# The copy of the input into the accumulator of the first expert layer, in one piece and in two halves

## The reference, cut to what matters

```
x = x + 0.5 * ffn(layernorm(x))
x = x + attention(layernorm(x))
x = x + 0.5 * ffn(layernorm(x))

ffn:  xn = x * rsqrt(mean(x*x) + eps) * norm_weight
      probs = softmax(xn @ router_w.T + router_b)
      gates, idx = top_k(probs.T, 2048)          # each of 8 experts takes its best 2048 rows
      ye = gelu(xn[idx] @ fc1.T + b1) @ fc2.T + b2
      out = scatter_add(ye * gates, idx) / sum of a row's gates
```

## Time and profile before

| what | value |
|---|---|
| median of 3 runs | 2059.93 us (2059.39 to 2060.3) |
| profiled execution | 2061.12 us |
| its span, first to last instruction | 2059.3 us |
| mean granted clock of TensorE in the span | 0.979 of 2.4 GHz |
| busy share: PE, DVE, ACT, POOL | 95%, 70%, 68%, 61% |

### The profile page before, as it was taken

One profiled execution on the slowest core, in us unless ns is written; L12 is line 12 of the kernel. 1 busy time (PEld: TensorE's weight loads), 2 busy tenths in 40 slices (PEclk: granted clock), 3 DMA queues, 4 the chain that ended last, 5 costly groups with the idle time before them and its releaser, 6 DMA issues.

```text
span 2059.3 us, 42658 instructions
## 1 busy us (share of the span) xinstructions
PE 1955.1 (95%) x15442; PEld 1358.3 (66%) x15442; DVE 1448.4 (70%) x4307; ACT 1399.0 (68%) x2680; POOL 1264.6 (61%) x1428
## 2 busy tenths in 40 slices
PE   8868999999999998799999999869999999999997
PEld 6635666666666665577777777536666666666665
DVE  7788877677777763489989998778655656556542
ACT  8645676666766764578888787556667666666663
POOL 8232788888888784544444443024887777766755
PEclk9979999999999999899999999989999999999999
DMA  9943555555657453556555554224565555655433
GB/s 288 336 143 100 101 101 98 119 98 106 107 94 129 73 81 62 103 121 162 160 159 145 155 149 113 96 72 116 101 121 101 101 102 95 130 93 100 74 60 42
DMA packets 361746, 242.34 MB, mean 118 GB/s; under 512 B 228929, under 2 KB 348993, under 8 KB 361281
## 3 DMA queue, kind: packets, MB, share of 16 engines
q1 hardware_dynamic: 304192, 172.34, 32.7%
q0 software_dynamic: 57344, 67.29, 21.6%
HBM read 121.03 MB, written 84.93 MB: 100 GB/s over the span
## 4 chain that ended last, share of the span: by engine, by line
PE 81%; DVE 5%; issue 5%; ACT 4%; POOL 2%; DMA 2%; SPq 1%; DVEq 0%; POOLq 0%; ACTq 0%
PE ps L1513 25%; PE ps L1514 25%; PE ps L1515 25%; ACT zt_l L734 2%; PE ps L1739 2%; ACT zt_h L734 1%; PE ps L1613 1%; PE ps L1686 1%; DVE bst L1015 1%; POOL xe L596 1%; PE ps L1768 1%; DMA xa<-x_d 0%; POOL out L618 0%; PE ps L1694 0%; PE ps L1731 0%
## 5 line engine op out<-in xcount | busy, mean ns | idle before, releaser
L1289 DVE SCALAR_TENSOR_TENSOR hid_l<-hf,hid_h 128x512 f16<-128x512 f32 x512 | 348.6, 691 | 310.2 <-ACT hid_h L734 308.9
L1513 PE MATMUL ps<-w_h,hid_h 128*128 128x256 f16 x2048 | 558.8, 273 | 3.9 <-DVE hid_l L1289 3.9
L1514 PE MATMUL ps<-w_l,hid_h 128*128 128x256 f16 x2048 | 558.8, 273 | 0.0
L1515 PE MATMUL ps<-w_h,hid_l 128*128 128x256 f16 x2048 | 558.8, 273 | 0.0
L834 ACT ACTIVATE hf<-ps,b 128x512 f32<-128x512 f32 x512 | 346.4, 677 | 137.8 <-PE ps L1515 105.8
L1513 PE MATMUL ps<-xt,w_h 128*128 128x512 f16 x1024 | 388.6, 380 | 13.5 <-ACT hf L834 9.1
L1515 PE MATMUL ps<-xt,w_l 128*128 128x512 f16 x1024 | 388.6, 379 | 0.0
L1514 PE MATMUL ps<-xt,w_h 128*128 128x512 f16 x1024 | 388.6, 379 | 0.0
L734 ACT ACTIVATE hid_h<-hf 128x512 f16<-128x512 f32 x512 | 322.4, 630 | 16.4
L608 POOL DMA_INDIRECT weight<-gate_d,gate_at x256 | 268.3, 1048 | 78.1 <-issue 74.4
L1513 PEld LDWEIGHTS ps<-w_h,hid_h 128*128 128x128 f16 x2048 | 200.7, 98 | 54.7 <-DVE hid_l L1289 4.7
(11 more groups left out here) (295 smaller groups left out, 4146.6 us busy)
## 6 DMA issues: line engine op xcount, KB each, us to landing
w_st<-fc_t SPq DMA_DIRECT2D x32, 1024.0 KB, 5.9
xin<-x SPq DMA_DIRECT2D x32, 512.0 KB, 6.0
xa<-x_d SPq DMA_DIRECT2D x32, 512.0 KB, 4.6
out<-x SPq DMA_DIRECT2D x32, 512.0 KB, 5.3
z_d<-z SPq DMA_DIRECT2D x32, 512.0 KB, 6.1
xt<-xs SPq DMA_TRANSPOSE x256
weight<-gate_d,gate_at POOLq DMA_INDIRECT x256
b_st<-fc_b SPq DMA_DIRECT2D x16, 128.0 KB
```

Source lines behind the costliest of these rows:

```text
L1289: dve.scalar_tensor_tensor(hid_l[:, n % 2, f, :], hf[:, f % HF, :], HS, hid_h[:, n % 2, f, :], ALU.mult, ALU.subtract).then_inc(s_hl, 1)
L1513: pe.matmul(dst, lh, rh, start=first, stop=False)
L1514: pe.matmul(dst, lh, rl, start=False, stop=False)
L1515: return pe.matmul(dst, ll, rh, start=False, stop=last)
```

## The change

The copy of x into `x1_d` is cut into two halves of 8192 rows, each one DMA with its own 16 increments of `s_copy`. The first is issued where the whole one was. The second is issued behind the transposes of chunk 1 and ahead of the first weights of the second expert. POOL waits for both.

```
+            def copied(half):
+
+                rows = slice(half * T // 2, (half + 1) * T // 2)
+                sp.dma_start(x1_d[rows].rearrange("(a b) d -> a (b d)", b=8), xf[rows].rearrange("(a b) d -> a (b d)", b=8)).then_inc(s_copy, 16)
...
                 if layer == 0:
-                    sp.dma_start(x1_d.rearrange("(a b) d -> a (b d)", b=8), xf.rearrange("(a b) d -> a (b d)", b=8)).then_inc(s_copy, 16)
+                    copied(0)
                     sp.wait_ge(s_tp, KD * NG)
                     sp.wait_ge(s_mv, NG // 2)
                 columns(N0)
                 columns(N0 + 1)
+                if layer == 0:
+                    copied(1)
                 w1_in(E0 + 1)
                 columns(N0 + 2)
                 w2_in(E0 + 1)
...
-                pool.wait_ge(s_copy, 16)
+                pool.wait_ge(s_copy, 16 * 2)
```

## The result

The changed kernel takes 2074.06 us (median of 4 runs, 2071.55 to 2076.14), the kernel before 2060.11 us on the same chip (4 runs, 2059.39 to 2061.52). The ratio is 1.0068, 95% interval 1.0056 to 1.0081: 14.0 us slower, where +13.8 was forecast. The profiled execution took 2076.14 us, with a span of 2074.4.

What follows compares the result with a forecast made beforehand. DVE was taken to bound the kernel until about 204 us, then PE. A 14.0 us delay in the first chunks less 0.15 us in the search made +13.8: median 2073.7 us, range 2064.0 to 2077.5.

Steps and rivals of the forecast that it cites:

- The search: Layer 0's search rounds: moving half the copy out gains 0.15 us, between 0 and 0.28.
- The load waits for the whole half: SP's queue: the second expert's first weights land only behind all 8 MiB, at 191.1 us instead of 164.3.
- L: Landing time of the second expert's first weight load: 191.1 us, ends 186.7 and 193.9.
- ACT stops, and DVE's order carries the delay: Chunk 1: ACT idle from 171.7 us until the load lands; DVE's turn 3 remainders shift 14.0 us, to 200.0.
- the margin: Turn 2 of chunk 1: ACT was 3.3 us ahead of DVE's remainders, which comes off the delay.
- The gather of chunk 3: POOL's queue: late under the copy, near 188 us, but hidden as DVE arrives at 198; its 2.75 us wait goes.
- rival A: Load overtakes or shares, landing before 175 us; only chunk 3's gather is late: +4.5 us, 2064.4; chance 0.11.
- Rival D: SP's issue stalls behind the copy, chunk 2's transposes come at 200 us or more: +18 to +20, 2079; chance 0.06.
- PE's clock: After PE's pause of some 15 us, the lower clock loses 2.3 us, covered by its 2.98 us wait: 0, at most 1.
- The chances: Forecast 0.74; slower by more than 4 us 0.87, no difference 0.10, faster 0.03.

Runs made afterwards that it cites:

- e8: Changed kernel, but both halves of the copy are issued at the whole copy's old place, none behind the transposes: 2061.48 us, ratio 1.0003.
- e4: Changed kernel, but the whole 16 MiB copy, as one DMA, stands behind the transposes of chunk 1, none in the search: 2098.98 us, ratio 1.0186.
- e1: Changed kernel, but the second half goes behind the load of the second expert's first weights instead of ahead of it: 2065.33 us, ratio 1.0021.
- e5: Changed kernel, but the second half is copied in separate pieces of 2 KB instead of 64 KB packets, same place: 2075.97 us, ratio 1.0075.
- e9: Changed kernel, but ACT issues the second half on its own queue in 2 KB pieces, 2.1 us before the weight load: 2071.61 us, ratio 1.0050.
- e3: Changed kernel, but the second DMA copies only the last quarter (4 MiB), the first three quarters (12 MiB): 2061.37 us, ratio 1.0008.
- e2: Changed kernel, but the second half goes behind the second expert's second weights, three places later: 2077.59 us, ratio 1.0088.
- e6: Changed kernel with the edits of e2 and e5: second half behind the second weights, in pieces of 2 KB: 2068.01 us, ratio 1.0038.
- e10: As e9, but the copy on ACT's queue has packets of 64 KB instead of pieces of 2 KB: 2083.62 us, ratio 1.0115.

## Why the prediction was right, point by point

- **The search** was to give 0.15 us, as half of the 0.28 us by which layer 0's is longer than layer 1's. It came out 0.14 us shorter, and that is luck: e8 has the whole copy beside the search and e4 none, and both are as short. The 0.28 us are not the copy's price, and what else they are stays open. The term is small, and the sum does not rest on it.
- **The load waits for the whole half, L = 191.1 us**: it landed at 190.95. Its closeness is in part luck, since terms inside were off and cancelled: the copy took 29.0 us from issue to landing where 25.2 and 1.6 for the gather were put down, the load landed 3.5 us behind it, not 5.3, and the copy was issued 0.5 us earlier. The 5.3 us were not those of an empty queue either: the transposes of chunk 1 were issued until 158.9 us, right ahead of that load. That the order on its queue makes it wait is shown by e1 (ahead of the copy: no wait), by e5 (other packets: the same wait) and by e9 (e5's packets, issued before the load, but on another queue: no wait).
- **ACT stops, and DVE's order carries the delay**: forecast 14.0 us at turn 3 of chunk 1 (200.0 us), measured 13.84 (199.81). ACT's wait was 19.6 us. DVE waited 16.59 us for ACT, 3.0 less, which is the margin (forecast 3.3), and 0.48 us more for the second half (0.6); the gather's 2.75 us are gone. e4 shows the slope above the threshold, e3 the threshold. Behind it the shift stays, as forecast: 15.5 us at the first scatter, 15.2 at the first round of layer 1's search (1327.17 against 1311.96), 15.1 at the end of the span.
- **The gather of chunk 3**: late, and hidden, as forecast. e1 and e2 show what it costs when nothing hides it: 4.7 and 17.0 us. e1 is rival A's case, priced at +4.5: a real mechanism that lay under the larger one. The rule from the Trainium skill's "DMA: Bandwidth & Descriptors", section "Queues, rings and completion order" (a DMA engine takes turns between queues by whole packets), agrees with e2 against e6 (24.13 against 7.26 us for the last of the four gathers) and with e10 against e9 (28.22 against 9.69 us of waiting for transposes); the forecast that the sum would not change by it held.
- **Rival D**: SP's issue was held, 20.66 us for four transposes, as D has it. But PE shows no wait for them; it stood until 192.73 us for ACT anyway, and began chunk 2 at 199.11. The price of D did not come.
- **PE's clock** was put at 0, at most 1 us. The first pause did cost nothing (217.90 - 204.05 is 13.85, no more than DVE's shift). But the next wait for DVE, 2.78 us and no longer than before, was followed by half speed this time, and cost 1.7 us in the profiled execution. That term was too small for this execution, but e8 had the same drop behind 3.16 us with no late load, while e3 and the kernel before had none behind 3.16 and 3.14 us. So the drop is not shown to be the change's. The granted clock of the four runs was 0.975 to 0.977 against 0.979 before, and the run with 0.977 is the shortest, 2071.55 us; that the spread of the runs is this clock is only argued from that.
- **The chances**: the prediction's 0.87 for a slower kernel is 0.86 by its own terms (0.74, 0.06 and half of 0.11). Nothing hangs on it.

## What to carry to other kernels

A large transfer that nobody waits for is free only where its queue has nothing behind it and the other queues have nothing urgent beside it: here it cost nothing that these runs can tell beside the search, 14 us ahead of a 1 MB load, and 17 us beside a gather. Before moving one, list what is issued behind it on its own queue until its bytes are through, and separately what other queues must land in that time. On its own queue only the place helps; against other queues small pieces help (a wait for a gather fell from 21 us to 4, one for transposes from 28 to 10).

## What the runs showed of the hardware

- A contiguous copy of 8 MiB from device memory to device memory moves in packets of 64 KB, and a gather of 128 rows on another queue, the last of four, took 24.13 us to land beside them (e2), 7.26 us beside pieces of 2 KB (e6), and 5.59 us beside a weight load (before).
- The pieces of 2 KB cost the copy itself next to nothing: 29.9 us to landing against 29.0 (e5, the changed kernel).
- A 1 MB load behind the copy on the same queue landed 18.1, 31.9 and 56.7 us after its issue, behind 4, 8 and 16 MiB (e3, the changed kernel, e4). Beside 8 MiB on another queue it went by 11 us after its issue with pieces of 2 KB (e9), and 26 to 30 us with 64 KB (e10).
- A wait of PE of about 3 us at one and the same step was followed by full speed in two executions (3.14 us before, 3.16 in e3) and by half speed in two others (3.16 us in e8, 2.78 in the changed kernel).
- SP's issue is held behind the copy: 20.66 us for four transposes behind 64 KB packets, instead of 5.13. Why it is held no row shows. Behind pieces of 2 KB the hold came one instruction earlier, at the weight load:

```profile
159.30 18.65 SPq L429 DMA_DIRECT2D w_st<-fc_t  x1
```
